# Four layer-norm variances: one fp32 product each, or two fp32r passes over a square that VectorE splits

## The chip, the cores and the metric

One Trainium2 chip, one core of it. The metric is the device time of one execution in microseconds (us), the median of several runs. Engines are named as the profile names them: PE is TensorE (PEld its weight loads), DVE is VectorE, ACT is ScalarE, POOL is GpSimd, SP is SyncE.

## What is computed

Two layers over `x` of shape (4, 1024, 128), each an attention-like part and a feed-forward part, and after each of the four parts a residual sum and a layer norm without gain:

```python
def _layernorm(x, axis=-1, eps=1e-05):
    m = jnp.mean(x, axis=axis, keepdims=True)
    v = jnp.var(x, axis=axis, keepdims=True)
    return (x - m) / jnp.sqrt(v + eps)

x = _layernorm(x + _L0_attn_ref(x, ...))   # norm 1: chunked delta rule, 4 heads of 32, chunk 32
x = _layernorm(x + _L0_ffn_ref(x, ...))    # norm 2: 8 experts of 256, top 2 of them gated
x = _layernorm(x + _L1_attn_ref(x, ...))   # norm 3: gated linear recurrence
x = _layernorm(x + _L1_ffn_ref(x, ...))    # norm 4: silu(x w1) * (x w2), two hidden 512x512, down to 128
```

Everything is fp32. The variance is what the change is about: the mean over the 128 features of the square of the centred value.

## The kernel before, in words

**Layout.** Features stand on the 128 partitions. The 1024 positions are cut into 8 tiles of 128 positions, times 4 sequences: a tile is 128x512. The mean over features is a matrix product with `mean_w`, a 128x128 matrix of 1/128, so its result stands on all partitions at once.

**Two kinds of product.** `mm` (line 318) issues one matmul. With plain fp32 operands it is recorded as two MATMUL instructions. `mm3` (line 321) is three fp32r matmuls for one product: each operand is held as a rounded part (`...h`) and the remainder (`...l`), and low by low is left out. The rounded part is made by a copy that casts to fp32r, the remainder by a subtraction. For most activations DVE makes the cast and POOL the subtraction; for some DVE makes both (`x1h`, `x1l` at lines 1181 and 1183, `x3h`, `x3l` at lines 1093 and 1095).

**Stages.** A first stage (to about 140 us) projects q, k, v of all tiles; then a triangular inverse (to about 210 us). The rest is a pipeline of four parts, in which one step works on several tiles at a time: `dense(m, a, f)` does the experts of tile m, the delta rule of tile a and the last product of the second feed-forward of tile f; `tails(f, m, a, l)` does the second feed-forward of f, norm 2, recurrence and norm 3 of m, and norm 1 and the router of a. `schedule` (line 216) calls them in turn, with the middle four rounds in a loop. Five `dense` calls have all three tiles, and six `tails` calls have f, m and a.

**What sets the order.** Each engine runs its own copy of `dense` and `tails` strictly in the order in which it is written, and the engines meet at semaphores. A layer norm walks over three engines: DVE centres (or sums, where the weights are centred already) and signals `d`; ACT squares (`square`, line 655; for norm 1 line 760) and signals `sq`; PE multiplies with `mean_w` (`var_product`, line 405) and signals `var`; ACT makes 1/sqrt as Exp(-0.5 Ln(v)) (lines 661 and 665); DVE scales (line 1033).

The four variance products stand in PE's program here: norm 2 in `tails` between `glu(f, 2)` and `glu(f, 3)` (line 542); norm 1 after `hidden(f, 2, O_H1...)` (line 566); norm 3 between two parts of the second hidden layer (line 580); norm 4 in the last expert of `dense`, between `down(m, 6)` and `down(m, 7)` (line 490). `glu(f, c)` on PE (line 503) makes the gate and the up product of chunk c; ACT applies SiLU (line 697); DVE multiplies (line 1126) and casts (line 1129); POOL subtracts (line 867). In the round of expert e of `dense`, DVE does: the subtraction `fbl` (line 1076), the cast `fbh` (line 1078), a piece of the delta rule (`delta_qp`, line 1046, or `delta_out`, lines 1055 and 1057), the gating `yg` of the expert before (line 1065), and after odd experts `delta_spread` (line 1039), for whose result `spread` PE waits in `delta_attn` (line 418). POOL subtracts `fbl` (line 850) and adds up `acc` (line 858).

Of the kernel before, what the change touches and what calls it, by code (L numbers as in the profile page):

```python
# [8 lines left out]
F32R = mybir.dt.float32r  # L9
# [7 lines left out]
NT = L // TOK  # L17
W = B * TOK
# [24 lines left out]
def build(nc, io):  # L43
    ctx = ExitStack()
    with ctx:
# [30 lines left out]
        eye = cst[:, C_EYE:C_EYE + 32]  # L76
        centre_w = sb("centre_w", [128, 128])
        sel = sb("sel", [128, E], F32R)
        s3row = sb("s3row", [128, 128]); wsum = sb("wsum", [128, 24])
# [20 lines left out]
        xt = sb("xt", [128, B, TOK + HALO])  # L100
        xv = xt[:, :, HALO:HALO + TOK]
        xth = sb("xth", [128, B, TOK + HALO], F32R); xtl = sb("xtl", [128, B, TOK + HALO], F32R)
        tb = sb("tb", [128, B, CN, C])
# [28 lines left out]
        tpr = opt[:, :].rearrange("p (i n) -> p i n", i=C)  # L132
        tpm = opt[:, :].rearrange("p (i h j) -> p h i j", h=NH, i=C)
        bank = [ps(f"bank{i}") for i in range(8)]

# [27 lines left out]
        for n in "1234":  # L163
            for k in ("d", "sq", "var", "rs", "x"):
                S[k + n] = sem(f"ln{n}_{k}")
        S["y3"], S["mu3"] = sem("ln3_y"), sem("ln3_mu")
# [150 lines left out]
        def _(pe):  # L317
# [86 lines left out]

            def var_product(n, t, src, bk):
                pe.wait_ge(S["sq" + n], t + 1)
                mm(bank[bk][:, :], mean_w, src[:, :]).then_inc(S["var" + n], 1)

# [55 lines left out]
            def dense(m, a, f):  # L464
                if a is not None:

                    pe.wait_ge(*after("lg_ready", a))
                    delta_wu(a, 0)
                for e in range(E):
                    if m is not None:  # L470
                        up(m, e)
                        gate_rows(m, e)
                    if e == 0 and f is not None:
                        output_product(f)
                    if a is not None:
                        (delta_state if e % 2 else delta_attn)(a, e // 2)
                    if a is not None and e == 4:

                        pe.wait_ge(S["x_in"], 16 * NT + 16 * a + 16)
                        mm(by_seq(bank[3][:, :]), wsm[:, 1, :], xv).then_inc(S["mixl_done"], 1)  # L480
                    if m is not None and e:
                        if f is not None and e == 1:
                            pe.wait_ge(*after("d4", f + 1))
                        down(m, e - 1)
                    if a is not None and e % 2 and e < E - 1:
                        delta_wu(a, e // 2 + 1)
                    if f is not None and e == E - 1:
                        if a is not None:
                            pe.wait_ge(*after("mix_act", a + 1))
                        var_product("4", f, f2, 3)  # L490
                if m is not None:
                    down(m, E - 1)
# [31 lines left out]
            def tails(f, m, a, l):  # L524
# [16 lines left out]
                if m is not None:  # L541
                    var_product("2", m, m2, 1)
                if f is not None:
# [20 lines left out]
                if a is not None:  # L564
                    pe.wait_ge(S["ors_done"], 2 * a + 2)
                    var_product("1", a, a2, 2)
                if f is not None:
# [11 lines left out]
                if m is not None:  # L579
                    var_product("3", m, m2, 1)  # L580
                if f is not None:
# [306 lines left out]
        def _(dve):  # L888
# [72 lines left out]
            dve.wait_ge(S["cst_in"], 16)  # L961
            V.tensor_copy(sel[:, :], cst[:, C_SEL:C_SEL + E])
            tt(centre_w[:, :], ident, mean_w, ALU.subtract).then_inc(S["cen_ready"], 1)
            dve.wait_ge(S["s3_row"], 1)
# [62 lines left out]
            def centre(n, t, buf, bk):  # L1027
                dve.wait_ge(S["mu" + n], t + 1)
                tt(buf[:, :], buf[:, :], bank[bk][:, :], ALU.subtract).then_inc(S["d" + n], 1)

            def scale(n, t, buf, rs, out):
                dve.wait_ge(*after("rs" + n, 2 * t + 2) if n in "34" else (S["rs" + n], 2 * t + 2))
                return tt(out[:, :], buf[:, :], rs[:, :], ALU.mult)
# [33 lines left out]
            def dense(m, a, f):  # L1067
                if a is not None:
                    delta_spread(a, 0)
                for e in range(E):  # L1070
# [25 lines left out]
                    if m is not None and e:  # L1096
                        gated(m, e - 1)
                    if a is not None and e % 2 and e < E - 1:
                        delta_spread(a, e // 2 + 1)
# [16 lines left out]
            def tails(f, m, a, l):  # L1116
# [27 lines left out]
                if F_:  # L1144
                    glu(0)
                    glu(1)
                    glu(2)
                    glu(3)
# [10 lines left out]
                if M_:  # L1159
# [3 lines left out]
                    dve.wait_ge(S["lru_a"], 2 * m + 1)  # L1163
                    ts(m4[:, :], m4[:, :], 1.0, -1e-19, ALU.subtract, ALU.min).then_inc(S["lru_m"], 1)
                    dve.wait_ge(S["lru_mult"], m + 1)
                    dve.wait_ge(S["lru_gx"], m + 1)
# [21 lines left out]
                if A_:  # L1188
# [17 lines left out]
                    for s in range(2):  # L1206
                        i = tt(gt2[:, :, s, :], rep(iota[:, :].rearrange("p (o e) -> p o e", o=1), 1, B),
                               rep(mf[:, :, s:s + 1], 2, E), ALU.is_equal)
                    i.then_inc(S["tk5"], 1)
                hi2(0)  # L1210
                hi2(1)
# [93 lines left out]
```

## Time and profile before

| | us |
|---|---|
| median of 3 runs (996.37 to 1002.29) | 1001.6 |
| the profiled execution, as timed | 1002.4 |
| its span in the trace | 1000.6 |
| PE busy in the span | 840.5 |
| DVE busy | 620.0 |
| ACT busy | 484.5 |
| POOL busy | 443.9 |

The 1.8 us between the profiled execution's time and its span lie outside the span. "Busy" of PE is modelled: consecutive matmuls overlap in the records, so what one costs in a dense stretch is the distance between starts. The pipeline of `dense` and `tails` runs from about 224 us to the end; one round of the loop takes 88.3 us, as between 610.61 and 698.88 us.

### The profile page before, as it was taken

To read this page: it belongs to the slowest core of one execution; us is meant where nothing else is said; L and a number is where in the kernel's file an instruction comes from. 1 tells how busy PE (TensorE), PEld (TensorE's weight loads), DVE (VectorE), ACT (ScalarE), POOL (GpSimd) and SP (SyncE) were. 2 spreads that over 40 slices of the span, in tenths; PEclk is the share of its full clock that TensorE was granted. 3 is DMA by queue.
4 is the path that set the end of the run, shared out by engine and by line. 5 is a ranking of instruction groups with operands and counts; after the bars stand their busy time and mean duration, and the time that the engine had idled before them with its cause. 6 is when DMAs were issued, how large, how long until landed. Compare 5 with 4: busy or idle time off the path is not lost.

```text
span 1000.6 us, 12264 instructions
## 1 busy us (share of the span) xinstructions
PE 840.5 (84%) x3874; PEld 643.0 (64%) x3874; DVE 620.0 (62%) x1182; ACT 484.5 (48%) x727; POOL 443.9 (44%) x339
## 2 busy tenths in 40 slices
PE   5999960028679679999999989999998999999986
PEld 3777750017458258678668857866785787676664
DVE  2343558983346466667768667776766677677452
ACT  3666632000234554664475466347446644766743
POOL 0534436991016216445435544543454454357343
PEclk9999965565569769999999999999999999999999
DMA  5244442001200200200200030020002000000000
GB/s 182 79 133 126 131 130 52 0 22 64 63 11 1 74 1 1 74 1 1 57 29 1 1 84 0 0 55 29 0 0 67 17 0 0 11 1 1 10 11 11
DMA packets 39974, 38.32 MB, mean 38 GB/s; under 512 B 1408, under 2 KB 34432, under 8 KB 39680
## 3 DMA queue, kind: packets, MB, share of 16 engines
q1 hardware_dynamic: 39936, 37.84, 13.0%
q8 instruction: 20, 0.33, 0.1%
q14 instruction: 18, 0.15, 0.0%
HBM read 23.16 MB, written 14.68 MB: 38 GB/s over the span
## 4 chain that ended last, share of the span: by engine, by line
PE 61%; DVE 11%; POOL 10%; ACT 9%; issue 7%; DMA 1%; ACTq 0%; POOLq 0%; DVEq 0%; SPq 0%
PE bank L319 60%; POOL opt L829 3%; POOL tmpg L826 3%; DVE m L1172 1%; DVE a L1107 1%; ACT L762 1%; POOL acc L858 1%; DVE sexp L1055 1%; POOL fbl L850 1%; POOL fbl L871 1%; POOL wml L831 1%; PE bank L382 1%; DVE yg L1065 1%; ACT m L765 1%; ACT m L767 1%
## 5 line engine op out<-in xcount | busy, mean ns | idle before, releaser
L850 POOL TENSOR_TENSOR fbl<-hf,fbh 128x512 fp32r<-128x512 f32 x64 | 83.2, 1301 | 133.7 <-DVE fbh L1078 133.7
L676 ACT ACTIVATE hf<-bank 128x512 f32<-128x512 f32 x64 | 38.4, 600 | 172.4 <-PE bank L319 171.1
L319 PEld LDWEIGHTS bank<-pk,spread 128*128 128x128 f32 x768 | 100.8, 211 | 23.9 <-issue 13.9
L319 PE MATMUL bank<-pk,spread 128*128 128x64 f32 x768 | 103.6, 295 | 13.1 <-issue 7.0
L871 POOL TENSOR_TENSOR fbl<-hf,fbh 128x512 fp32r<-128x512 f32 x32 | 44.2, 1380 | 105.8 <-DVE fbh L1134 105.8
L858 POOL TENSOR_TENSOR acc<-acc,yg 128x512 f32<-128x512 f32 x48 | 66.4, 1383 | 45.0 <-DVE yg L1065 45.0
L1076 DVE TENSOR_TENSOR fbl<-hf,fbh 128x512 fp32r<-128x512 f32 x64 | 61.8, 966 | 39.3 <-ACT fbh L678 39.3
L808 POOL TENSOR_TENSOR spread<-pk,cst 128x1024 f32<-128x1024 f32 x16 | 40.4, 2544 | 85.8 <-DVE pk L935 85.8
L319 PE MATMUL bank<-fal,wfh 128*128 128x512 f32 x160 | 65.8, 411 | 2.5 <-ACT hf L703 1.6
L867 POOL TENSOR_TENSOR fal<-hf,fah 128x512 fp32r<-128x512 f32 x32 | 41.7, 1304 | 53.4 <-DVE fah L1129 53.4
L1065 DVE TENSOR_TENSOR yg<-bank,gb 128x512 f32<-128x512 f32 x64 | 43.8, 684 | 32.1 <-PE bank L319 32.1
L319 PE MATMUL bank<-fbl,wmh 128*128 128x512 f32 x128 | 57.6, 450 | 7.1 <-DVE yg L1065 6.6
L703 ACT ACTIVATE hf<-bank,vec 128x512 f32<-128x512 f32 x64 | 42.3, 687 | 42.7 <-PE bank L319 42.6
L319 PE MATMUL bank<-fbl,wfh 128*128 128x512 f32 x128 | 58.9, 460 | 4.7 <-POOL fbl L871 4.7
L319 PE MATMUL bank<-fah,wfh 128*128 128x512 f32 x160 | 62.5, 390 | 0.0
L319 PE MATMUL bank<-fah,wfl 128*128 128x512 f32 x160 | 62.4, 390 | 0.0
L392 PE MATMUL bank<-cst,opt 128*128 128x128 f32 x32 | 6.4, 352 | 65.1 <-POOL opt L829 63.6
L879 POOL TENSOR_TENSOR fal<-hf,fah 128x512 fp32r<-128x512 f32 x32 | 41.6, 1301 | 43.1 <-DVE fah L1134 43.1
L841 POOL TENSOR_TENSOR texp<-tb,cst 128x512 f32<-128x512 f32 x28 | 35.5, 1279 | 45.1 <-DMA tb<-tt 45.1
L319 PE MATMUL bank<-x1l,wmh 128*128 128x512 f32 x128 | 54.7, 427 | 0.0
L319 PE MATMUL bank<-fbh,wfh 128*128 128x512 f32 x128 | 52.6, 411 | 0.0
L319 PE MATMUL bank<-fbh,wfl 128*128 128x512 f32 x128 | 52.4, 410 | 0.0
(213 smaller groups left out, 2298.3 us busy)
## 6 DMA issues: line engine op xcount, KB each, us to landing
pack<-pk SPq DMA_DIRECT2D x8, 1280.0 KB, 6.0
pk<-pack SPq DMA_DIRECT2D x8, 1280.0 KB, 7.2
xt<-in_xh SPq DMA_DIRECT2D x16, 262.0 KB, 3.0
ws<-in_wf SPq DMA_DIRECT2D x8, 352.0 KB, 3.2
stg<-in_wm SPq DMA_DIRECT2D x1, 2048.0 KB, 8.0
tt<-ttc SPq DMA_DIRECT2D x1, 2048.0 KB, 6.3
out<-f SPq DMA_DIRECT2D x8, 256.0 KB, 2.9
tb<-tt SPq DMA_DIRECT2D x7, 256.0 KB, 7.3
```

Source lines behind the costliest of these rows:

```text
L319: return P.matmul(out, lhsT, rhs, start=start, stop=stop, skip_group_check=skip)
L676: A.activation(hf[:, 0, :], bank[4][:, :], ACT.Gelu).then_inc(S["gelu_done"], 1)
L703: A.activation(hf[:, o % 2, :], bank[4 + o][:, :], ACT.Gelu, scale=vec[:, v + o:v + o + 1])\
L808: G.tensor_tensor(kspread[g][:, :, :, :], rep(pks[s][:, g * 8:(g + 1) * 8, SK:SK + 1, :], 2, NH), heads(8), ALU.mult).then_inc(S["kexp_don ...
L841: G.tensor_tensor(texp[:, n % 2, :, :, :], rep(src[:, :, n:n + 1, :], 2, NH), heads(B), ALU.mult)\
L850: G.tensor_tensor(fbl[:, s, :], hf[:, 1, :], f32(fbh[:, s, :]), ALU.subtract)\
L858: G.tensor_tensor(acc[:, :], (x1 if e == 1 else acc)[:, :], yg[:, (e - 1) % 2, :], ALU.add)\
L867: G.tensor_tensor(fal[:, c, :], hf[:, c % 2, :], f32(fah[:, c, :]), ALU.subtract)\
L871: G.tensor_tensor(fbl[:, o, :], hf[:, o % 2, :], f32(fbh[:, o, :]), ALU.subtract)\
L879: G.tensor_tensor(fal[:, o, :], hf[:, o % 2, :], f32(fah[:, o, :]), ALU.subtract)\
L1065: tt(yg[:, e % 2, :], bank[6][:, :], gb[:, e % 2, :], ALU.mult).then_inc(S["yg_ready"], 1)
L1076: tt(fbl[:, s, :], hf[:, 0, :], f32(fbh[:, s, :]), ALU.subtract).then_inc(S["lo0"], 1)
```

## The change

The square of each norm is split by DVE into `vh` (cast to fp32r) and `vl` (remainder, also fp32r), and PE makes the variance in two fp32r matmuls against `mean_r`, an fp32r copy of the matrix of 1/128. One pair `vh`, `vl` serves all four norms, so a split waits until PE has read the one before. It lies over the buffer `xth` of the first stage, which is free by then.

```diff
+        mean_r = sb("mean_r", [128, 128], F32R)
...
+        vh, vl = over("vh", [128, W], F32R, at_xth), over("vl", [128, W], F32R, at_xth + 2112)
...
-            def var_product(n, t, src, bk):
-                pe.wait_ge(S["sq" + n], t + 1)
-                mm(bank[bk][:, :], mean_w, src[:, :]).then_inc(S["var" + n], 1)
+            def var_product(n, t, bk):
+                pe.wait_ge(S["sp" + n], 2 * t + 2)
+                mm(bank[bk][:, :], mean_r[:, :], vl[:, :], stop=False)
+                mm(bank[bk][:, :], mean_r[:, :], vh[:, :], start=False).then_inc(S["var" + n], 1)
...
+            V.tensor_copy(mean_r[:, :], mean_w)
             tt(centre_w[:, :], ident, mean_w, ALU.subtract).then_inc(S["cen_ready"], 1)
...
+            def split_square(n, t, src):
+
+                dve.wait_ge(S["sq" + n], t + 1)
+                V.tensor_copy(vh[:, :], src[:, :]).then_inc(S["sp" + n], 1)
+                dve.wait_ge(S["sp" + n], 2 * t + 1)
+                tt(vl[:, :], src[:, :], f32(vh[:, :]), ALU.subtract).then_inc(S["sp" + n], 1)
...
+                    if f is not None and e == 5:
+                        if a is not None or m is not None:
+                            dve.wait_ge(S["var3"], f + 2)
...
+                        split_square("4", f, f2)
                     if a is not None and e % 2 and e < E - 1:
                         delta_spread(a, e // 2 + 1)
...
                     glu(0)
                     glu(1)
+                if M_:
+                    if L_:
+                        dve.wait_ge(S["var4"], l + 1)
...
+                    split_square("2", m, m2)
+                if F_:
                     glu(2)
                     glu(3)
...
                     ts(m4[:, :], m4[:, :], 1.0, -1e-19, ALU.subtract, ALU.min).then_inc(S["lru_m"], 1)
+                if A_:
+                    if M_:
+                        dve.wait_ge(S["var2"], m + 1)
+                    split_square("1", a, a2)
+                if M_:
                     dve.wait_ge(S["lru_mult"], m + 1)
...
                     i.then_inc(S["tk5"], 1)
+                if M_:
+                    if A_:
+                        dve.wait_ge(S["var1"], a + 1)
...
+                    split_square("3", m, m2)
                 hi2(0)
                 hi2(1)
```

PE's four `var_product` calls stay where they were. On DVE the splits are put between instructions that stood next to each other.

DVE in the loop's `tails`, norm 2. Before (`hf` and `fah` are the product and its cast of one glu chunk; these are chunks 1 and 2, lines 1126 and 1129):

```order
L1121 REGISTER_ALU
L1126 SCALAR_TENSOR_TENSOR hf<-bank,vec,gb 128x512
L1129 CAST fah<-hf 128x512
L1121 REGISTER_ALU
L1126 SCALAR_TENSOR_TENSOR hf<-bank,vec,gb 128x512
L1129 CAST fah<-hf 128x512
```

and now (`m_88` is `m2`, the square; the changed file's lines 1147 and 1150 are 1126 and 1129 of before):

```order
L1142 REGISTER_ALU
L1147 SCALAR_TENSOR_TENSOR hf<-bank,vec,gb 128x512
L1150 CAST fah<-hf 128x512
L1040 CAST vh<-m_88 128x512
L1041 ISA
L1042 TENSOR_TENSOR vl<-m_88,vh 128x512
L1142 REGISTER_ALU
L1147 SCALAR_TENSOR_TENSOR hf<-bank,vec,gb 128x512
L1150 CAST fah<-hf 128x512
```

The cast and the subtraction of the square have moved in ahead of chunk 2.

DVE in a whole `dense`, expert 5 and the start of expert 6, norm 4. Before (`yg` is the gating of expert 4, `spread` is `delta_spread`, `fbl` is the subtraction for expert 6):

```order
L1065 TENSOR_TENSOR yg<-bank,gb 128x512
L1037 REGISTER_ALU
L1039 TENSOR_TENSOR spread<-bank,cst 128x1024
L1074 ISA
L1076 TENSOR_TENSOR fbl<-hf,fbh 128x512
```

and now:

```order
L1078 TENSOR_TENSOR yg<-bank,gb 128x512
L1040 CAST vh<-f_92 128x512
L1041 ISA
L1042 TENSOR_TENSOR vl<-f_92,vh 128x512
L1050 REGISTER_ALU
L1052 TENSOR_TENSOR spread<-bank,cst 128x1024
L1087 ISA
L1089 TENSOR_TENSOR fbl<-hf,fbh 128x512
```

`spread` now comes after both instructions of the split. ACT's and POOL's programs have as many rows as before, in the same order.

## Rows read from the trace of the kernel before

**Rows 1.** The page: span and busy time of each engine.

```profile
span 1000.6 us, 12264 instructions
PE 840.5 (84%) x3874; PEld 643.0 (64%) x3874; DVE 620.0 (62%) x1182; ACT 484.5 (48%) x727; POOL 443.9 (44%) x339
```

**Rows 2.** The chain of waits, one loop round: start us, us, what.

```profile
677.20 1.28 ACT L736
...
683.33 3.70 PE bank L319 x8
...
698.88 11.92 PE bank L319 x46
```

**Rows 3.** Timeline of PE and ACT around norm 2's product: start, duration.

```profile
674.73 1.02 PE L319 MATMUL bank<-m,cst 128*128 128x512 f32 x2
675.83 0.39 PE L319 MATMUL bank<-x3h,wfl 128*128 128x512 f32 x1
676.05 0.40 PE L319 MATMUL bank<-x3h,wfh 128*128 128x512 f32 x1
676.49 0.69 ACT L697 ACTIVATE gb<-bank,vec 128x512 f32<-128x512 f32 x1 [1.56 <-PE bank L319]
```

**Rows 4.** Timeline of DVE and POOL there, glu chunk 1.

```profile
673.95 0.97 DVE L1129 CAST fah<-hf 128x512 fp32r<-128x512 f32 x1
675.00 1.30 POOL L867 TENSOR_TENSOR fal<-hf,fah 128x512 fp32r<-128x512 f32 x1 [0.36 <-DVE fah L1129]
```

**Rows 5.** Groups by line: cast and subtraction of `x3` on DVE.

```profile
L1093 DVE CAST x3h<-x 128x512 fp32r<-128x512 f32 x8 | 3.4, 428 | 0.3
L1095 DVE TENSOR_TENSOR x3l<-x,x3h 128x512 fp32r<-128x512 f32 x8 | 5.5, 692 | 0.3
```

**Rows 6.** Timeline: two SBUF instructions of DVE, POOL between them.

```profile
665.88 0.68 DVE L1104 TENSOR_TENSOR a<-oT,pk 128x512 f32<-128x512 f32 x1
666.12 1.59 POOL L858 TENSOR_TENSOR acc<-acc,yg 128x512 f32<-128x512 f32 x1 [0.91 <-DVE yg L1065]
666.59 1.66 DVE L1107 SCALAR_TENSOR_TENSOR a<-a,a 128x512 f32<-128x512 f32 x1
```

**Rows 7.** Timeline of expert 5's end: DVE, POOL, and PE waiting for `spread`.

```profile
743.63 0.68 DVE L1065 TENSOR_TENSOR yg<-bank,gb 128x512 f32<-128x512 f32 x1
744.23 1.21 DVE L1039 TENSOR_TENSOR spread<-bank,cst 128x1024 f32<-128x1024 f32 x1
744.47 1.29 POOL L858 TENSOR_TENSOR acc<-acc,yg 128x512 f32<-128x512 f32 x1 [0.90 <-DVE yg L1065]
745.57 1.99 PE L319 MATMUL bank<-pk,spread 128*128 128x64 f32 x16
```

**Rows 8.** Timeline around norm 3's product, in two rounds.

```profile
701.76 1.32 DVE L1207 TENSOR_TENSOR gt<-iota,mf 128x32 f32<-128x32 f32 x2
703.32 1.02 PE L319 MATMUL bank<-m,cst 128*128 128x512 f32 x2
523.64 0.50 PE L319 MATMUL bank<-fbl,wfh 128*128 128x512 f32 x1 [0.64 <-POOL fbl L871]
526.81 1.02 PE L319 MATMUL bank<-m,cst 128*128 128x512 f32 x2
```

**Rows 9.** Timeline around norm 1's product, and the end of norm 4's.

```profile
690.30 0.43 DVE L1164 TENSOR_SCALAR m<-m 128x512 f32<-128x512 f32 x1 [2.28 <-ACT m L765]
692.20 0.69 DVE L1167 SCALAR_TENSOR_TENSOR m<-m,m 128x512 f32<-128x512 f32 x1 [1.47 <-ACT m L772]
697.18 1.06 PE L319 MATMUL bank<-wr,x 128*128 128x8 f32 x8 [0.22 <-DVE x1l L1183]
754.40 0.47 PE L319 MATMUL bank<-fbl,wmh 128*128 128x512 f32 x1 [0.65 <-DVE yg L1065]
```

**Rows 10.** Stretches: us, busy PE, PEld, DVE, ACT, POOL, PEclk, DMA, GB/s.

```profile
696.00:700.00 4.00, 3.14 (x15) 2.02 (x14) 3.88 (x12) 1.95 (x4) 2.10 (x2) 0.95 0.00 0
700.00:704.00 4.00, 4.00 (x12) 2.93 (x11) 3.44 (x13) 1.17 (x2) 3.17 (x4) 0.62 0.00 0
```

More of the change, by code:

```diff
@@ L101, in build @@
         xv = xt[:, :, HALO:HALO + TOK]
+        at_xth = top[0]
         xth = sb("xth", [128, B, TOK + HALO], F32R); xtl = sb("xtl", [128, B, TOK + HALO], F32R)
@@ L163, in build @@
         for n in "1234":
-            for k in ("d", "sq", "var", "rs", "x"):
-                S[k + n] = sem(f"ln{n}_{k}")
+            for k in ("d", "sq", "sp", "var", "rs", "x"):
+                if k + n not in ("d1", "x3"):
+                    S[k + n] = sem(f"ln{n}_{k}")
         S["y3"], S["mu3"] = sem("ln3_y"), sem("ln3_mu")
@@ L489, in dense @@
                             pe.wait_ge(*after("mix_act", a + 1))
-                        var_product("4", f, f2, 3)
+                        var_product("4", f, 3)
                 if m is not None:
@@ L541, in tails @@
                 if m is not None:
-                    var_product("2", m, m2, 1)
+                    var_product("2", m, 1)
                 if f is not None:
@@ L565, in tails @@
                     pe.wait_ge(S["ors_done"], 2 * a + 2)
-                    var_product("1", a, a2, 2)
+                    var_product("1", a, 2)
                 if f is not None:
@@ L579, in tails @@
                 if m is not None:
-                    var_product("3", m, m2, 1)
+                    var_product("3", m, 1)
                 if f is not None:
@@ L1097, in dense @@
                         gated(m, e - 1)
+                    if f is not None and e == 5:
+                        if a is not None or m is not None:
+                            dve.wait_ge(S["var3"], f + 2)
+                        elif isinstance(f, int) and f == NT - 2:
+                            dve.wait_ge(S["var3"], NT)
+                        else:
+                            dve.wait_ge(S["var4"], f)
+                        split_square("4", f, f2)
                     if a is not None and e % 2 and e < E - 1:
@@ L1146, in tails @@
                     glu(1)
+                if M_:
+                    if L_:
+                        dve.wait_ge(S["var4"], l + 1)
+                    elif isinstance(m, int) and m == 1:
+                        dve.wait_ge(S["var3"], m)
+                    split_square("2", m, m2)
+                if F_:
                     glu(2)
@@ L1209, in tails @@
                     i.then_inc(S["tk5"], 1)
+                if M_:
+                    if A_:
+                        dve.wait_ge(S["var1"], a + 1)
+                    else:
+                        dve.wait_ge(S["var2"], m + 1)
+                    split_square("3", m, m2)
                 hi2(0)
```

## The prediction

> **What bounds the kernel now.** I read four views, in this order. The page says that PE is busy 84% of the span and DVE 62% [rows 1], which alone would make any relief of PE look good. The chain of waits over one loop round says where PE really ends last [rows 2]: the long unbroken PE pieces are the second half of the hidden layers and `dense` (698.88 to about 750 us), but in the 25 us before 698.88 the chain hops from PE to ACT (677.20), back to PE (683.33) and then over ACT, DVE and POOL. In that half a saving on PE counts only if the instruction that waits for it is the next link. Then the timeline around each of the four variance products, to see what PE does directly before and after, and what DVE does where a split is put in. Last the stretches with PE's granted clock.
>
> **What is saved.** The fp32 product of norm 2 starts at 674.73, and the second pass of the product behind it at 675.83; passes of fp32r stand 0.23 us apart (675.83, 676.05) [rows 3]. So the fp32 product takes 675.83 - 674.73 - 0.23 = 0.87 us of PE, and two fp32r passes will take 0.46: a saving of 0.41 us. There are 4 norms x 8 tiles = 32 products, 13.1 us if every one lay on the path and the clock was full.
>
> **What is added.** For each product DVE casts the square (0.43 us) and subtracts (0.69 us), by the same pair on `x3` [rows 5]; with the semaphore between them 1.15 us. That is 32 x 1.15 = 37 us of DVE work, and PE's wait moves from ACT's square to the end of DVE's subtraction. The cast of `mean_r` in the prologue is a quarter of such a cast; I count it at nothing. What matters is where each split stands in DVE's queue.
>
> **The two instructions meet POOL.** DVE's `a<-oT,pk` (both inputs in SBUF) ends at 666.56 [rows 6]; POOL's sum, issued at 666.12 during it, takes 1.59 us and ends at 667.71, although it takes 1.29 alone [rows 7]; and DVE's next instruction, issued at 666.59, takes 1.66 instead of 0.69 and ends at 668.25, 0.54 after POOL's. They take turns, whole instruction by whole instruction. A cast shows the same: 0.97 us [rows 4] where it takes 0.43 alone [rows 5]. An instruction of DVE that reads the bank, as `spread<-bank` at 744.23, does not hold up POOL's sum at 744.47, which keeps its 1.29 [rows 7]. So a split that is issued when POOL has just been released costs DVE 0.43, then POOL's 1.28, then 0.56: about 2.3 us and not 1.15. The Trainium skill (SBUF — State Buffer, "Who interferes with whom") says that GpSimd and VectorE share one port pair under an exclusive lock, taken for a whole instruction, and that a copy in a two-port mode and an instruction with two SBUF inputs both take it. By that rule every split beside POOL costs the 2.3 us, and only by free durations would it cost 1.15; the trace agrees with the rule.
>
> **Norm 2** (7 times beside a glu). DVE's cast of chunk 1 ends at 674.92 and releases POOL at 675.00 [rows 4]. The new cast goes first (to 675.4), POOL next (to 676.7), the subtraction ends at 677.3. PE was at its product at 674.73 and now starts at 677.35: 2.6 us later, less 0.41 saved, 2.2. Behind it on PE is glu chunk 3, and ACT has waited 1.56 us for exactly that [rows 3]; then ACT runs its table loads and exponentials without a gap until PE goes on at 683.33 [rows 2]. So nothing takes the 2.2 back. Without POOL in between it is 1.0. Queued behind the split on DVE is glu chunk 2; its remainder is due at PE only in the third group of hidden passes, some 4 us later, so that is covered. Sum 7 x 2.2 = 15.4. The first one (334.96 us, no glu, half clock) I put at 0.
>
> **Norm 4** (expert 5). Each `yg` releases a sum on POOL: `yg` ends at 744.31, the sum starts at 744.47, and `spread` runs beside it to 745.44. PE takes `spread` up at 745.57, with next to no slack [rows 7]. Now the cast goes first (744.78), the sum to 746.06, the subtraction to 746.6, `spread` to 747.8. PE stands still for 2.3 us in the stretch where it is the bound; without POOL 1.15. The saving does not come back: behind norm 4's product PE waits 0.65 us for DVE's `yg` anyhow [rows 9], and would wait 1.06. Five whole `dense` give 5 x 2.3 = 11.5. Of the three others, the one without a delta rule (913 us) runs on DVE and POOL turn by turn: +1.8. At 957 us the split comes behind `x3l` in DVE's queue and the next glu behind it on PE: 1.15 + 0.46 = +1.6. The last one lies in the open chain to the output: 1.15 - 0.41 = +0.7. Together 15.6.
>
> **Norm 3.** The split follows `gt<-iota,mf`, which ends at 703.08 [rows 8]; POOL is idle then, so it ends at 704.25, and PE starts at 704.30 instead of 703.32: +0.98 - 0.41 = 0.57. This round is helped by a slow clock: PE had 0.62 of it in 700 to 704 us [rows 10]. Where the clock was full PE reached the product 3.17 us after the restart behind `fbl` (523.64 to 526.81), in place of 4.44 (698.88 to 703.32) [rows 8], while DVE's router work takes its 5.4 us either way: +2.2 - 0.41 = 1.8. Four rounds of the first kind, two of the second: 5.9. The first norm 3 (358 us) delays the gate by its 1.15, the last one little (0.3). Together 7.3.
>
> **Norm 1.** The split fits between 690.73 and 692.20, where DVE waits 1.47 us for ACT [rows 9]: 1.15 us, POOL idle, 0.3 us of slack. PE finishes 0.41 us sooner and then waits longer for `x1l` (0.22 us now) [rows 9]. Zero, except +0.4 for the first (275 us), which is alone and at half clock.
>
> **Sum:** 15.4 + 15.6 + 7.3 + 0.4 = 38.7 us. On the profiled execution (1002.4 us: span 1000.6 and 1.8 around it) that is 1041; the median of the runs shown is 0.8 lower, so I forecast 1040 us. ACT and POOL run the same instructions, and no transfer is moved; SP's loads follow the tile and have slack.
>
> **Rivals.**
> 1. *The turns with POOL do not happen*, because the gap between cast and subtraction is too short for POOL to get in, or it comes late. Then norm 2 is 7 x 1.0 and norm 4 is 5 x 1.15 + 1.15 + 1.6 + 0.7: 7.0 + 9.2 + 7.3 + 0.4 = 23.9, 1025 us. For it: the gap is some 0.03 us. Against it: 666.56 to 666.59, where 0.03 us was enough [rows 6].
> 2. *The clock falls as well.* PE gets two new stops of over 2 us per round. After the weak stretch before 700 us (the small router products, 0.22 and 0.64 us idle) the granted clock fell from 1.0 to 0.62 over 700 to 704 us, that is to 1.2 of 2.4 GHz for most of it [rows 10], and passes stood 0.43 apart instead of 0.23: some 1.5 us lost per fall. Five stops in `dense` at 1.5 and seven in `tails` at about 0.9 (part of it beside ACT) add up to 14: 1054 us. For it: the new stops are three times as long as those. Against it: PE's stops today, of 0.65 us and less, are passed at full clock wherever the work between them is full-sized [rows 8, 9]. The Trainium skill (TensorE: Matmul & The Clock Gate, "HAM oscillation") says that idle gaps throttle the engine again and that the work behind them pays; it speaks for this rival, and the fall after 700 us agrees with it.
> 3. *PE is the bound nearly everywhere and DVE has room* (its 62%). Then the splits hide, PE's two dropped half-products count, and the time falls by up to 13.1 us, to 989. For it: 60% of the chain is PE. It decides from the point at which each split ends before PE arrives; that point is missed by 2.6 us in norm 2 [rows 4] and 2.3 in norm 4 [rows 7], and met in norm 1 alone [rows 9]. If it held for norms 2 and 4 by half, the time would be as before.
>
> **How the numbers follow.** The forecast as worked out has 0.55 (own range 1032 to 1047), rival 1 0.15, rival 2 0.20, rival 3 0.10, of which 0.04 for faster by over 1% and 0.06 for no change; 1% is about what a measurement of this kernel can tell from none. Slower has 0.55 + 0.15 + 0.20 = 0.90. The range takes in rivals 1 and 2, less the last of each: 1023 to 1056.
>
> **What would show it.** Right: DVE's group of casts of `vh` at about 0.43 us, the subtractions of `vl` with a mean near 1.1 us because about half of them stand behind POOL; PE waiting for `vl` by over 2 us before norm 2's product, and over 2 us for `spread` before expert 6's small products; norm 1 without a new wait; a loop round of 88.3 + 2.2 + 2.3 + 0.6 = 93.4 us or more. Rival 1: subtractions of 0.69 throughout, a round of 91. Rival 2: stretches behind the stops at a clock of 0.5 to 0.7, a round over 95. Wrong as a whole: a round of 88 us or less, with PE's product of norm 2 starting as soon as chunk 2's products are through.

## The result and the profile after

The changed kernel takes 1042.9 us (median of 4 runs, 1042.28 to 1047.21), the kernel before 1001.9 beside it (4 runs): a ratio of 1.0429, with a 95% interval of 1.0381 to 1.0478. The profiled execution of the changed kernel took 1043.5 us. The kernel before took 996 to 999 us in some of its runs and 1000 to 1003 us in the others, and its trace is of one of 1002.4 us, so a comparison of spans or pieces with that trace can differ by up to 5 us from the ratio of the medians.

The page of the changed kernel, span and busy times:

```profile
span 1041.7 us, 12359 instructions
PE 837.6 (80%) x3874; PEld 645.5 (62%) x3874; DVE 664.4 (64%) x1247; ACT 484.5 (47%) x727; POOL 445.1 (43%) x339
```

Against [rows 1] the span is 41.1 us longer. PE is busy 2.9 us less and DVE 44.4 us more, yet DVE is still idle for over a third of the span: the page alone does not say where the 41 us are. The groups of the new instructions do (line, engine, operation; shapes; count, busy us, mean ns; idle time before them and its releaser):

```profile
L1042 DVE TENSOR_TENSOR vl<-m,vh 128x512 fp32r<-128x512 f32 x16 | 17.8, 1113 | 0.5
L1042 DVE TENSOR_TENSOR vl<-f,vh 128x512 fp32r<-128x512 f32 x8 | 11.3, 1417 | 0.3
L1042 DVE TENSOR_TENSOR vl<-a,vh 128x512 fp32r<-128x512 f32 x8 | 5.5, 693 | 0.3
L1040 DVE CAST vh<-a 128x512 fp32r<-128x512 f32 x8 | 3.4, 422 | 4.5 <-ACT a L765 4.5
L323 PE MATMUL bank<-vl,mean_r 128*128 128x512 f32 x32 | 16.4, 514 | 40.4 <-DVE vl L1042 40.4
```

The same subtraction takes 0.693 us in norm 1 (`a`), 1.417 in norm 4 (`f`), and 1.113 as a mean over norms 2 and 3 (`m`): of those 16, the seven of norm 2 beside a glu take 1.64 to 1.67 and the other nine 0.69. PE has idled 40.4 us for `vl`; not all of it is new, for PE's waits for `m`, ahead of norm 3's mean product, fell from 6.5 to 2.7 us. The list of waits, by releaser (sum, count, longest), adds the second new one:

```profile
PE bank L323 <- DVE vl L1042: 40.4, 19, 4.9
PE bank L323 <- DVE spread L1052: 16.6, 10, 2.1
```

Before, PE waited 5.3 us in 4 places for `spread`. And the chain of waits over two rounds of the loop (start, us, what):

```profile
638.80 13.88 PE bank L323 x79
...
674.13 1.22 DVE spread L1052
...
693.52 1.65 DVE vl L1042
...
724.68 0.70 DVE vl L1042
...
734.27 13.88 PE bank L323 x79
829.67 13.91 PE bank L323 x79
```

A round is 734.27 - 638.80 = 95.5 us, and the next 95.4, against 88.3. (From gate product to gate product the four rounds are 92.8, 94.9, 95.5 and 95.4 us, against 86.3, 88.2, 88.3 and 88.3.) Three links are new: DVE's splits of norms 2 and 3, and `spread` behind the split of norm 4.

**Norm 2.** PE, DVE, POOL and ACT in the timeline of the changed kernel, glu chunks 1 and 2:

```profile
598.68 0.97 DVE L1150 CAST fah<-hf 128x512 fp32r<-128x512 f32 x1
599.57 0.42 DVE L1040 CAST vh<-m 128x512 fp32r<-128x512 f32 x1
599.73 1.38 POOL L872 TENSOR_TENSOR fal<-hf,fah 128x512 fp32r<-128x512 f32 x1 [0.36 <-DVE fah L1150]
600.02 1.64 DVE L1042 TENSOR_TENSOR vl<-m,vh 128x512 fp32r<-128x512 f32 x1
601.72 0.49 PE L323 MATMUL bank<-vl,mean_r 128*128 128x512 f32 x1 [2.10 <-DVE vl L1042]
603.18 0.69 ACT L702 ACTIVATE gb<-bank,vec 128x512 f32<-128x512 f32 x1 [3.53 <-PE bank L323]
603.25 0.63 PE L323 MATMUL bank<-x3h,wfl 128*128 128x512 f32 x1
603.68 0.63 PE L323 MATMUL bank<-x3h,wfh 128*128 128x512 f32 x1
```

POOL's instruction is issued at 599.73, 0.29 us before DVE's subtraction, and runs first; the subtraction takes 1.64 us. PE stops for 2.10 us, and ACT behind it waits 3.53 us for glu chunk 3, where it waited 1.56 [rows 3]. From 603.25 on PE's passes are 0.43 us apart (603.25, 603.68), where they were 0.23 apart before [rows 3]: the clock has fallen behind the stop. The stretch after it in the changed kernel (us, busy of PE, PEld, DVE, ACT, POOL, PEclk, DMA share, GB/s) shows a mean of 0.68, a mixture of the full level and the lower one of 1.2 GHz:

```profile
604.00:608.00 4.00, 4.00 (x13) 3.15 (x13) 1.18 (x2) 3.97 (x5) 1.45 (x2) 0.68 0.00 0
```

**Norm 4.** The same engines at the end of expert 5:

```profile
671.51 0.68 DVE L1078 TENSOR_TENSOR yg<-bank,gb 128x512 f32<-128x512 f32 x1
672.10 0.42 DVE L1040 CAST vh<-f 128x512 fp32r<-128x512 f32 x1
672.35 1.31 POOL L863 TENSOR_TENSOR acc<-acc,yg 128x512 f32<-128x512 f32 x1 [0.91 <-DVE yg L1078]
672.55 1.66 DVE L1042 TENSOR_TENSOR vl<-f,vh 128x512 fp32r<-128x512 f32 x1
674.13 1.21 DVE L1052 TENSOR_TENSOR spread<-bank,cst 128x1024 f32<-128x1024 f32 x1
```

`spread` starts 2.62 us after `yg` instead of 0.60 [rows 7], and PE waits 2.13 us for it before the small products at 675.47. The same stop one round earlier, and the stretch behind that one:

```profile
675.47 1.99 PE L323 MATMUL bank<-pk,spread 128*128 128x64 f32 x16 [2.13 <-DVE spread L1052]
580.61 1.99 PE L323 MATMUL bank<-pk,spread 128*128 128x64 f32 x16 [2.13 <-DVE spread L1052]
580.00:584.00 4.00, 3.39 (x20) 3.09 (x21) 1.90 (x5) 0.00 (x0) 1.29 (x1) 0.83 0.00 0
```

Behind the stop at 580.61 the clock falls (from 582.41 to 585.33 the passes are 0.43 us apart); behind the other four stops of this kind it does not.

**Norm 3.** PE, with DVE's split:

```profile
723.03 0.39 PE L323 MATMUL bank<-fbh,wfh 128*128 128x512 f32 x1
724.23 0.42 DVE L1040 CAST vh<-m 128x512 fp32r<-128x512 f32 x1
724.68 0.69 DVE L1042 TENSOR_TENSOR vl<-m,vh 128x512 fp32r<-128x512 f32 x1
725.42 0.50 PE L323 MATMUL bank<-vl,mean_r 128*128 128x512 f32 x1 [2.00 <-DVE vl L1042]
726.38 0.63 PE L323 MATMUL bank<-fbh,wfl 128*128 128x512 f32 x1
726.81 0.63 PE L323 MATMUL bank<-fbh,wfh 128*128 128x512 f32 x1
```

and stretches of the same kernel (columns as above):

```profile
720.00:724.00 4.00, 3.31 (x12) 2.10 (x12) 3.85 (x18) 1.23 (x2) 3.64 (x4) 1.00 0.00 0
724.00:728.00 4.00, 2.58 (x7) 2.11 (x8) 3.93 (x8) 3.27 (x6) 2.37 (x3) 0.75 0.00 0
728.00:732.00 4.00, 4.00 (x16) 3.19 (x15) 0.96 (x4) 0.85 (x1) 0.45 (x1) 0.82 0.00 0
```

This one differs from [rows 8, 10]. The router's products before it are now followed by a stretch at clock 1.00, so PE comes to the product early and stands for 2.00 us; the clock falls only behind that stop, where passes are 0.43 us apart (726.38, 726.81) for some 3 us.

**The round in four pieces.** The six rounds that do norms 2 and 3, cut at the starts of four products on PE that both kernels have, and summed:

| from ... to (what the change touches in it) | before | after | difference |
|---|---|---|---|
| head product (`head_w`, in `tails`) to router products (norm 2, and norm 1) | 147.6 | 162.0 | +14.4 |
| router products to gate product (norm 3) | 72.9 | 82.3 | +9.4 |
| gate product to `xt` by `wsm` (nothing) | 133.7 | 133.7 | 0 |
| from there to the next head product, five times (norm 4) | 119.0 | 130.6 | +11.6 |
| the rest of the span: first and last tiles | | | +5.7 |

By single rounds, in order, the first row is +1.65, +2.6, +2.6, +3.0, +2.9, +1.65, the second +2.2, +1.9, +0.6, +2.2, +2.2, +0.4, and the fourth +2.05, +3.4, +2.05, +2.05, +2.04. The piece without a split has not moved by 0.1 us. The experiments are read in these pieces; they are below called the norm 2 piece, norm 3 piece, and norm 4 piece.

### The profile page after: what moved, and what is told of

Same layout as the page of the kernel before. It is cut to its first block, busy times and chain, and to the rows that moved or that the text cites. A ratio compares the mean times of both kernels' runs of the same rounds, so it can differ in the third digit from the quotient of the medians.

```text
span 1041.7 us, 12359 instructions
## 1 busy us (share of the span) xinstructions
PE 837.6 (80%) x3874; PEld 645.5 (62%) x3874; DVE 664.4 (64%) x1247; ACT 484.5 (47%) x727; POOL 445.1 (43%) x339
## 4 chain that ended last, share of the span: by engine, by line
PE 52%; DVE 18%; issue 10%; POOL 9%; ACT 9%; DMA 1%; DVEq 0%; ACTq 0%; POOLq 0%; SPq 0%
PE bank L323 52%; POOL opt L834 3%; POOL tmpg L831 3%; DVE vl L1042 2%; DVE sexp L1068 1%; DVE m L1205 1%; DVE spread L1052 1%; ACT L767 1%; POOL acc L863 1%; DVE yg L1078 1%; DVE hf L1147 1%; POOL fbl L855 1%; POOL wml L836 1%; DVE a L1128 1%; DVE vh L1040 1%
## 5 line engine op out<-in xcount | busy, mean ns | idle before, releaser
L813 POOL TENSOR_TENSOR spread<-pk,cst 128x1024 f32<-128x1024 f32 x16 | 40.4, 2544 | 85.6 <-DVE pk L940 85.6
L323 PE MATMUL bank<-fbl,wfh 128*128 128x512 f32 x128 | 54.5, 426 | 4.7 <-POOL fbl L876 4.7
L846 POOL TENSOR_TENSOR texp<-tb,cst 128x512 f32<-128x512 f32 x28 | 35.8, 1292 | 44.4 <-DMA tb<-tt 44.4
```

What stands on the lines that cost most here:

```text
L323: return P.matmul(out, lhsT, rhs, start=start, stop=stop, skip_group_check=skip)
L813: G.tensor_tensor(kspread[g][:, :, :, :], rep(pks[s][:, g * 8:(g + 1) * 8, SK:SK + 1, :], 2, NH), heads(8), ALU.mult).then_inc(S["kexp_don ...
L846: G.tensor_tensor(texp[:, n % 2, :, :, :], rep(src[:, :, n:n + 1, :], 2, NH), heads(B), ALU.mult)\
```

## The experiments

Twelve kernels ran, in three groups of four with runs of the kernel before beside each group (medians 1001.5, 997.7 and 998.5 us). So times of different groups are compared by their ratio to before, given with its 95% interval; the changed kernel itself stands at 1.0429. Pieces are read from the traces.

**One norm at a time goes back.** The theory is that the cost is the sum of three stops of PE. The three kernels `e1_n4_old`, `e2_n2_old` and `e3_n3_old` differ in one string, "4", "2" or "3"; `e4_n1_only` has "234":

```diff
+OLD = "4"
...
             def var_product(n, t, bk):
+                if n in OLD:
+                    pe.wait_ge(S["sq" + n], t + 1)
+                    mm(bank[bk][:, :], mean_w, dict(zip("1234", (a2, m2, m2, f2)))[n][:, :]).then_inc(S["var" + n], 1)
+                    return
...
             def split_square(n, t, src):
+                if n in OLD:
+                    return
```

`e1_n4_old`:

> Norm 4 goes back to one fp32 product and no split; norms 1 to 3 keep the split. Theory (each split costs what it makes PE wait at its own place): norm 4 was priced at 15.6 us, so about 1042.9 - 15.6 = 1027 us, 1.025 times the kernel before, and PE's stop of 2.1 us before the small products behind spread is gone. Rival A (the splits cost as DVE work, whichever norm they belong to; 41 us in four equal parts): 1042.9 - 10.3 = 1033 us. Rival B (most of the loss is a slower clock that any stop brings): more than 20 us come back, under 1023 us.

Measured: 1029.3 us, 1.0287 [1.0246, 1.0329]. That is near the 1027 expected. The norm 4 piece is back to 119.0 us exactly and the round is 92.4 us. But two pieces that were not touched moved: norm 3's rose from 82.3 to 85.9, and norm 2's fell from 162.0 to 159.0. The falls of the clock have changed places: behind norm 2's stops the passes now stay 0.23 us apart, and they are 0.43 apart behind norm 3's stop in five rounds of six.

`e2_n2_old`:

> Norm 2 goes back to one fp32 product and no split; the others keep it. Theory: norm 2 was priced at 15.4 us (7 products beside a glu, 2.2 us each), so 1042.9 - 15.4 = 1027.5 us, perhaps 2 to 4 us less because the granted clock now falls behind those stops. Rival A (equal parts of DVE work): 1033 us.

Measured: 1026.6 us, 1.0269 [1.0228, 1.0309]. As expected (1027.5, ratio 1.026); the norm 2 piece is back to 147.7 us, and norm 3's is unchanged at 82.3.

`e3_n3_old`:

> Norm 3 goes back to one fp32 product and no split; the others keep it. Theory: norm 3 was priced at 7.3 us, so about 1035.5 us. Rival A (equal parts): 1033 us. Rival B (norm 3 costs nothing because its wait only fills time in which the clock was low anyway): 1042.9 us.

Measured: 1029.7 us, 1.0321 [1.0264, 1.0378]: a miss. Norm 3 gives back 11 us by the ratios and 13 by the medians, not the 7.4 expected. The total alone would not exclude 7.4, but the norm 3 piece falls by 13.3 us, to 69.0, below its 72.9 of before. The 3.9 us below are the slow clock that the kernel before had ahead of this product [rows 10]: four of its rounds have 12.6 us in this piece and the two with a full clock 11.3, and here five of six have 11.3. The other 9.4 are what the split cost; the forecast had this norm undersized.

`e4_n1_only`:

> Only norm 1 is split; norms 2, 3 and 4 have their fp32 product. Theory: the split of norm 1 lies in DVE's wait for ACT and costs 0.4 us in all, so the kernel before plus 0.4: 1002.3 us, ratio 1.000. Rival A (equal parts of DVE work): 1002 + 10.3 = 1012 us, ratio 1.010.

Measured: 1002.4 us, 1.0023 [1.0004, 1.0041], 0.2% above the 1.000 expected; the trace shows none of it. All four pieces are at their values of before within 0.1 us, although DVE makes the split of norm 1 eight times; rival A (1012 us) is refuted. PE's wait for `x1l` rose from 0.22 to 0.60 us, as forecast: what the shorter product saves is waited there. In ratio to before the three steps back are 1.4, 1.6 and 1.1%, together 4.1% against 4.3% lost: nearly additive, with norm 1 at about nothing.

**One split is moved.** If the cost is the place in DVE's queue and not the work, the same instructions elsewhere cost nothing. `e5_n4_late` puts the split behind `spread`:

```diff
+                    if a is not None and e % 2 and e < E - 1:
+                        delta_spread(a, e // 2 + 1)
                     if f is not None and e == 5:
...
                         split_square("4", f, f2)
-                    if a is not None and e % 2 and e < E - 1:
-                        delta_spread(a, e // 2 + 1)
```

> As the changed kernel, but in expert 5 DVE makes spread first and the split of norm 4 behind it. The same instructions, the same waits, one place later. Theory (what costs is that spread stands behind the split, and that POOL's sum gets in between): PE's stop before the small products of expert 6 (2.13 us) goes in five dense calls, 5 x 2.1 to 2.3 = 11 us, so 1032 us. The split is then covered by PE's 5 us of work up to the next thing that it needs from DVE. Rival A (DVE work costs wherever it stands): 1043 us.

Measured: 1033.9 us, 1.0336 [1.0286, 1.0386]. The timeline of DVE and POOL there:

```profile
668.85 0.68 DVE L1078 TENSOR_TENSOR yg<-bank,gb 128x512 f32<-128x512 f32 x1
669.45 1.22 DVE L1052 TENSOR_TENSOR spread<-bank,cst 128x1024 f32<-128x1024 f32 x1
669.69 1.29 POOL L863 TENSOR_TENSOR acc<-acc,yg 128x512 f32<-128x512 f32 x1 [0.92 <-DVE yg L1078]
670.58 0.69 DVE L1040 CAST vh<-f 128x512 fp32r<-128x512 f32 x1
671.30 0.69 DVE L1042 TENSOR_TENSOR vl<-f,vh 128x512 fp32r<-128x512 f32 x1
```

`spread` reads the bank and runs beside POOL's sum; by the time the split comes, POOL is nearly through, the subtraction takes 0.69, and the norm 4 piece is 119.1 us: as before, with all of the split's work still there. So the place costs and not the work. The two steps of the forecast's norm 4 (the turns and the want of slack at `spread`) go together with this move; it does not price them apart. The total fell by 0.9% (9 us) and not by the piece's 11.5, for norm 3's piece rose to 86.0 and norm 2's fell to 158.7, as in `e1_n4_old`. Behind norm 2's stop (at 598.06) the clock now stays full:

```profile
600.00:604.00 4.00, 4.00 (x19) 3.31 (x18) 1.18 (x2) 3.95 (x6) 1.83 (x2) 1.00 0.00 0
```

`e6_n2_early` puts norm 2's split one glu chunk earlier:

```diff
                     glu(0)
+                if M_:
...
+                    split_square("2", m, m2)
+                if F_:
                     glu(1)
```

> As the changed kernel, but in tails DVE splits norm 2's square after glu chunk 0 in place of chunk 1. Theory of the turns with POOL: POOL is then busy ahead of the cast only, and idle at the subtraction, since chunk 1 is not cast yet; the split ends at about 1.7 us before its end now, so each of 7 tails calls is 1.7 us shorter, 11.9 us, 1031 us; the subtractions of norm 2 take 0.69 us each and not 1.66. Rival 1 (no turns; position alone): the split moves ahead by one chunk, 1.1 us, so 7 x 1.1 = 7.7 us, 1035 us. Rival C (chunk 1, now behind the split, becomes the late one): no gain, 1043 us.

Measured: 1032.3 us, 1.0328 [1.0281, 1.0374]. The norm 2 piece falls from 162.0 to 151.0. DVE, POOL and PE there:

```profile
594.55 1.29 POOL L872 TENSOR_TENSOR fal<-hf,fah 128x512 fp32r<-128x512 f32 x1 [5.63 <-DVE fah L1150]
594.65 1.47 DVE L1040 CAST vh<-m 128x512 fp32r<-128x512 f32 x1 [0.19 <-ACT m L662]
596.16 0.69 DVE L1042 TENSOR_TENSOR vl<-m,vh 128x512 fp32r<-128x512 f32 x1
596.90 0.50 PE L323 MATMUL bank<-vl,mean_r 128*128 128x512 f32 x1 [0.81 <-DVE vl L1042]
```

Now the cast stands behind POOL (1.47 instead of 0.42), the subtraction runs free, and 0.81 us of PE's wait is left of 2.10. The cast started as soon as ACT's square was done, so it can't come earlier; with a free cast (0.42) PE would by these rows hardly wait, an estimate that no run here tests. So the turns are there (1.47 for the cast, 0.69 for the subtraction), but they cost on the other instruction, and the move saves 1.3 us of PE's wait in a round and not 1.7. The other 3 us of the 11.0 in the piece are the falls of the clock behind this stop, which are gone here. Rival C is refuted; the gain by itself would not tell the theory from rival 1. The norm 4 piece, where nothing was changed, rose from 130.6 to 135.3: now two of its stops have a fall of the clock behind them.

`e7_n3_early` puts norm 3's split ahead of the router's work:

```diff
                 hi1(3)
+                if M_:
...
+                    split_square("3", m, m2)
                 if A_:
...
                     i.then_inc(S["tk5"], 1)
-                if M_:
...
-                    split_square("3", m, m2)
```

> As the changed kernel, but DVE splits norm 3's square ahead of the router's work (before lg is copied) and not behind it. Theory: vl is ready before PE arrives, norm 3's wait on PE (2.0 us at the longest, 0.7 at the shortest) goes, and the router's result, 2.4 us later, is still in time for PE or nearly: 5 to 8 us back, 1036 us. Rival C (the gate becomes what PE waits for): nothing back, 1043 us or more.

Measured: 1044.8 us, 1.0457 [1.04, 1.0515]: a miss, and no gain at all. Yet the move did its work. PE no longer waits before the product, and the norm 3 piece fell from 82.3 to 70.6, by 11.7 us. The norm 4 piece rose by 10.6, to 141.2. PE's small products behind `spread` in this kernel, and the stretches around them:

```profile
671.76 3.47 PE L323 MATMUL bank<-pk,spread 128*128 128x64 f32 x16 [2.14 <-DVE spread L1052]
```

```profile
668.00:672.00 4.00, 1.86 (x9) 1.21 (x9) 3.97 (x5) 2.07 (x4) 1.31 (x1) 1.00 0.00 0
672.00:676.00 4.00, 4.00 (x19) 3.81 (x19) 1.05 (x4) 0.00 (x0) 1.26 (x1) 0.50 0.00 0
676.00:680.00 4.00, 4.00 (x15) 3.22 (x13) 0.69 (x1) 0.81 (x2) 1.12 (x1) 0.65 0.00 0
```

The stop is the same as in the changed kernel, 2.14 us against 2.13. There the clock stayed full behind it:

```profile
672.00:676.00 4.00, 1.87 (x11) 1.28 (x9) 3.97 (x6) 2.07 (x4) 1.31 (x1) 1.00 0.00 0
676.00:680.00 4.00, 4.00 (x26) 3.52 (x25) 1.46 (x4) 0.27 (x1) 1.40 (x2) 1.00 0.00 0
```

Here it fell to 0.50, the lower level of 1.2 GHz: the group of 16 small products takes 3.47 us instead of 1.99. Four of the five stops of this kind have such a fall behind them, where it was one in the changed kernel: three norm 4 pieces are longer by 3.0 us each, and the one that had a fall already by 1.6. So the gain was eaten by the clock at another stop.

**Both moves at once** is the test of that reading. `e9_n3_n4` joins the edits of `e5_n4_late` and `e7_n3_early`, which leaves no stop at norm 4 for the clock to fall behind:

> The two moves together: split 3 ahead of the router, split 4 behind spread; norm 2 as in the changed kernel. Alone the early split 3 gave nothing (1044.8), though in its trace PE no longer waits for vl there. Theory: what it gave was lost again behind norm 4's stop, where the granted clock was 0.50 for some 7 us and spread's products took 3.4 us instead of 2.0; with that stop gone there is no such fall, and split 3's gain shows on top of the late split 4: 1034 less 6 to 10 us, 1024 to 1028 us. Rival (moving split 3 is worth nothing in itself): 1034 us.

Measured: 1017.4 us, 1.0183 [1.016, 1.0207], better than expected. In ratio to the changed kernel the two moves alone give -0.9% and +0.3%, and together -2.4%. The norm 3 piece is 69.8 us, the norm 4 piece 119.0, and three of the four rounds are 88.7. What is left is the norm 2 piece, 159.3.

`e10_all_moved` adds norm 2's move:

> All three moves: split 2 behind glu chunk 0, split 3 ahead of the router, split 4 behind spread. Theory: the gains add, 10 us for norm 2 on top of the run before, 1014 to 1018 us; still above the kernel before, since norm 2's product waits for its split by about 0.9 us net and PE's saving lies where PE waits anyway. Rival 3 (with the stops gone PE's shorter products count): at or below the kernel before, 1001 us or less.

Measured: 1008.1 us, 1.0084 [1.0064, 1.0105], again better than expected. The pieces are 151.1, 71.3 and 119.1. The same 32 splits and 64 passes, in other places of DVE's program, cost 0.8% here, 8 to 10 us, where they cost 4.3% there. PE at norm 2 here:

```profile
586.61 0.50 PE L323 MATMUL bank<-vl,mean_r 128*128 128x512 f32 x1 [0.82 <-DVE vl L1042]
```

It is still not faster than before: the norm 2 piece keeps 3.5 us (PE's 0.82 of wait is more than the 0.41 that a product saves), the norm 3 piece gains 1.6, and the rest, about 3.5 of the 5.6 us of span over the trace of before, is in the first and last tiles.

**No split at all.** What is PE's saving worth when nothing is added? In `e8_one_pass`, made from the kernel before, ACT writes the square as fp32r (norms 1 and 4 into one buffer, 2 and 3 into another) and PE makes one pass over it. The remainder of the square is left out of the variance, so this kernel computes something less exact; how much less, no run here measures.

```diff
-                mm(bank[bk][:, :], mean_w, src[:, :]).then_inc(S["var" + n], 1)
+                w, x = (mean_r[:, :], vr[n]) if n in ONE else (mean_w, src)
+                mm(bank[bk][:, :], w, x[:, :]).then_inc(S["var" + n], 1)
...
+                dst = vr[n] if n in ONE else dst
                 A.activation(dst[:, :], src[:, :], ACT.Square).then_inc(S["sq" + n], 1)
```

> The kernel before, with ACT writing each square rounded to fp32r and PE making the variance in one fp32r pass; the remainder of the square is left out, and DVE has no split. PE loses 0.64 us per product, 20.5 us in all, and nobody gets more work. Theory (PE's saving counts only where PE's product is the next link): norm 2 gives 7 x 0.64 through ACT, norm 3 6 x 0.64, the last norm 4 0.64 and the first products at half clock about 3: some 12 us, 990 us, ratio 0.988; norms 1 and 4 give nothing because PE waits for DVE right behind them. Rival 3 (PE is the bound nearly everywhere): 20 us, 981 us, ratio 0.980.

Measured: 992.8 us, 0.994 [0.9919, 0.996], by 0.6% faster than before, half of the 12 us expected. All its runs (991.5 to 993.8) lie under all those of the kernel before (996.0 to 1002.9). PE's products are shorter by 32 x 0.64 = 20 us, of which 6 us show by the ratio; against the trace of before, of 1002.4 us, the span is 10.9 us shorter. In the traces the norm 2 and norm 3 pieces are 3.8 us shorter each, and the norm 4 piece is 119.1, so nothing. Norm 2's is 0.62 to 0.65 in every round, the saving of one product; norm 3's runs from -1.9 to +0.65, for there the falls of the clock move too. ACT's square takes 0.629 us with either output (`m`, 16 of them, in both traces).

`e11_one_pass_14` does this for norms 1 and 4 alone, `e12_one_pass_23` for norms 2 and 3 (the string `ONE`):

> One fp32r pass over squares that ACT rounds, for norms 1 and 4 alone; their remainder is left out; norms 2 and 3 keep the fp32 product. PE loses 16 x 0.64 = 10 us of work. Theory (behind these two products PE waits for DVE anyway): 1 to 2 us, from the first and the last alone, ratio 0.998 to 0.999. Rival 3: 10 us, ratio 0.990.

Measured: 1002.3 us, 1.0032 [1.0019, 1.0046]. No gain, and by its interval not the 0.998 to 0.999 expected. Its twelve runs take 1001.2 to 1003.3 us, those of the kernel before beside it 996.8 to 1002.9, and its trace has the same span as the trace of before, 1000.6 us.

> The same for norms 2 and 3 alone; norms 1 and 4 keep the fp32 product. PE loses as much work, 10 us. Theory (the next link hangs on norm 2's product through ACT, and on norm 3's through PE): nearly all of what the one pass gave for all four norms, 7 to 9 us, ratio 0.992. Rival: the two halves are alike, ratio 0.997 each.

Measured: 993.6 us, 0.9937 [0.9917, 0.9958]: all of the gain, with the norm 2 and norm 3 pieces at 143.9 and 69.1 (143.8 and 69.1 in `e8_one_pass`). PE behind norm 1 in `e11_one_pass_14`:

```profile
607.53 1.06 PE L324 MATMUL bank<-wr,x 128*128 128x8 f32 x8 [0.60 <-DVE x1l L1191]
```

PE waits 0.60 us for `x1l` where it waited 0.22 [rows 9]: 0.38 of the 0.64 us that norm 1's product saves. The router products start where they did: the piece is 147.7, and it was 147.6.

## Why the prediction was right

The time (1040 us, measured 1042.9) and the direction were right, and so was the mechanism for norms 2 and 4 (the split behind POOL, and the next link behind it). But part of the agreement of the sums is luck: the stops cost less than forecast, falls of the clock that the forecast did not count made up for it, and norm 3 and the first and last tiles were off in opposite directions.

- **The turns with POOL** came as argued: 1.64 and 1.66 us for the subtraction beside POOL, 0.69 free, with the cast at 0.42, the pattern of [rows 6]. The pair takes 2.1 us, where 2.3 was forecast. Rival 1 (a gap of 0.03 us is too short) is refuted by these rows. `e5_n4_late` shows the other side: behind `spread` the subtraction takes 0.69, and the cast 0.69 too, still with the end of POOL's sum beside it. The Trainium skill (SBUF — State Buffer, "Who interferes with whom") describes an exclusive port lock held for a whole instruction; the 1.64 and 0.69 of one instruction agree with it.
- **Norm 2**, forecast 2.2 us in each of six rounds with a glu, 13.2 in these: the piece grew by 14.4. The sum hides two parts. The stop alone costs 1.6 in the first and the last of the six rounds (PE's wait is 1.75 there) and 2.0 in the four between, as `e5_n4_late` shows, where the clock stays full behind it: 11.1 in six rounds, 2 less than forecast. In the changed kernel the clock falls behind the stop in those four rounds (603.25, 603.68), which adds 0.6 to 1.0 each, some 3.2 in all. That is rival 2's mechanism at about its price (0.9).
- **Norm 4**, forecast 11.5 us for five whole `dense`: 11.6, and `e5_n4_late` takes all of it away. Four of them grew by 2.05 and not by 2.3; the fifth grew by 3.4, since the clock falls behind its stop (580.61). The exact sum is luck.
- **Norm 1**, forecast 0 in the rounds: 0, shown by `e4_n1_only`, with the longer wait for `x1l` that was forecast.
- **Norm 3 is the step that failed**: "four rounds of the first kind" at 0.57 us each. The forecast took the slow clock that preceded the product in four rounds [rows 10] as given, a cover under which PE would arrive late anyway. In the changed kernel the fall comes behind the new stop instead in three of these four: the piece went from 12.6 to 14.8 us (+2.2). In the fourth the fall still comes ahead of the product (626.99 to 629.92), PE waits 0.75 us, and the piece went to 13.2 (+0.6, as forecast). The two rounds with a full clock before gave +1.9 and +0.4, where 1.8 was forecast for each; the +1.9 came another way than forecast, by a fall ahead of the product and a wait of 0.73, and in the last round PE waits only 0.52. That makes 9.4 in six rounds in place of 4 x 0.57 + 2 x 1.8 = 5.9. A wait cannot be set against a clock dip that may move when the work before it changes.
- **First and last tiles** were forecast at 8.1 us and measured at 5.7 with everything else that is outside the pieces. This hid part of the miss in norm 3: the four rounds from gate product to gate product grew by 6.6 to 7.2 us where 5.1 was forecast.
- **Rival 2** (the clock falls as well) holds in part, and the forecast gave it too little room beside its own case. Behind norm 4's stops the clock fell once in five in the changed kernel; behind those of norm 2 it fell in four rounds of six, behind those of norm 3 in three. By its own mark, a round over 95 us, the rounds of 95.5 and 95.4 just pass; by the time (1054) it did not come. The Trainium skill (TensorE: Matmul & The Clock Gate, "HAM oscillation") tells of idle gaps that throttle the engine again, in a kernel whose waits are longer than the stops here. The falls in `e7_n3_early` look like it at 2.14 us, and the stop of 2.13 us at 675.47 has none: a stop of this length may be followed by a fall, and need not be.
- **Rival 3** (PE is the bound nearly everywhere) is refuted by `e8_one_pass`: even a saving with nothing added shows 6 us of 20 by the ratio, and norms 2 and 3 alone give all of it (`e12_one_pass_23`).

What stays open is why the clock falls behind one stop of 2.1 us and not behind the same stop in another kernel, or in another round of the same kernel. That was not isolated; the runs only show that the falls move when work before them moves.

## What to carry to other kernels

Work put on an engine that is idle for over a third of the span can still cost more than it saves: ask which instruction stands directly behind it in that engine's queue, who waits for that, and whether POOL has just been released, because the pair then takes 2.1 us and not 1.15. Moving the same splits behind what PE waits for, or one chunk ahead, brought the loss from 4.3% to 0.8%. Norm 3's move paid only together with norm 4's, since alone the clock took its gain back at the next stop: try such moves together before one is dropped. If a value rounded to fp32r is exact enough, let the engine that writes it write it so: here that took ACT no extra time, and it was the only way that ended faster than before. It leaves out the remainder, and what that does to the result has to be judged by itself.

## What was not expected of the hardware

- A gain can be taken back in a place that the edit does not touch: in `e7_n3_early` -11.7 us in one piece and +10.6 in another, with the same stop (2.13 and 2.14 us) followed once by clock 1.00 and once by 0.50.
- Less work on PE need not pay at all: `e11_one_pass_14` has two norms' products 0.64 us shorter each, and against the median of before it is 0.3% slower, with an interval that excludes no change. Its trace is as long as that of before (1000.6 us): the norm 3 piece is 1 us longer (73.9 against 72.9, all of it in the last round), the norm 2 and norm 4 pieces are the same within 0.1, and the rest is 1 us shorter. Where the 0.3% come from is open.
- The one that stands behind pays: beside norm 2's split, where POOL runs first, its subtraction took 1.38 us against 1.30 before [rows 4], and DVE's 1.64 against 0.69; in [rows 6] POOL was issued behind an instruction of DVE and took 1.59 against 1.29.
